# Two tiles for a blocked inverse, and a merge step put in another order, in a two-layer AdaLN kernel

## What is computed

```python
h = layernorm(x) * (1 + ca) + sa
qkvz = h @ W_qkvz                       # per key head: q, k, 2 v, 2 z of 128 columns
q, k, v = silu(causal_conv4(q, k, v))   # four taps along the sequence
beta = sigmoid(b); alpha = exp(-exp(A_log) * softplus(a + dt_bias))
q, k = l2norm(q) / sqrt(128), l2norm(k)
def step(S, q_t, k_t, v_t, a_t, b_t):   # scan over 256 positions
    S = S * a_t
    v_new = (v_t - S^T k_t) * b_t
    S = S + outer(k_t, v_new)
    return S, S^T q_t
og = o * silu(z)
og = og * rsqrt(mean(og * og) + 1e-6) * norm_weight
x = x + ga * (og @ W_out)
```

## Time and profile before

| | us |
|---|---|
| median of 3 runs | 1217.29 (1217.04 to 1225.51) |
| profiled execution | 1213.53 |
| its span in the trace | 1211.8 |
| PE busy | 1089.0 (90%) |
| DVE busy | 957.2 (79%) |
| ACT busy | 808.4 (67%) |
| POOL busy | 733.3 (61%) |

### The profile page before, as it was taken

The page is one execution under the profiler, slowest core; times in us unless marked ns, Lnnn a source line. Parts: engine busy times, 40 slices in busy tenths (PEclk is TensorE's granted clock), DMA queues, the critical chain, the costliest instruction groups (busy, mean ns, idle before and its releaser), DMA issues. The chain is left out here.

```text
span 1211.8 us, 29974 instructions
## 1 busy us (share of the span) xinstructions
PE 1089.0 (90%) x10488; PEld 948.9 (78%) x10488; DVE 957.2 (79%) x2560; ACT 808.4 (67%) x2225; POOL 733.3 (61%) x1186
## 2 busy tenths in 40 slices
PE   6684799999999999999999999999998888999985
PEld 6583688988888888889898888888887776776754
DVE  6888689898989899999989898989982435328754
ACT  6342576777777777877777777777775764219873
POOL 3274677777777776787778777777777512014111
PEclk9886999999999999999999999999998999999988
DMA  5221226323131313132222313131314130011000
GB/s 186 65 60 36 86 48 73 58 67 80 45 90 41 82 43 106 35 90 56 68 57 68 90 41 83 41 82 33 72 39 126 34 105 1 1 37 39 2 19 18
DMA packets 140869, 72.79 MB, mean 60 GB/s; under 512 B 114184, under 2 KB 130064, under 8 KB 138800
## 3 DMA queue, kind: packets, MB, share of 16 engines
q1 hardware_dynamic: 140720, 70.88, 23.0%
HBM read 57.06 MB, written 13.78 MB: 58 GB/s over the span
## 5 line engine op out<-in xcount | busy, mean ns | idle before, releaser
L1076 POOL TENSOR_TENSOR Tn<-Tn,tmp 64x31 f32<-64x31 f32 (+15 forms) x496 | 280.3, 565 | 38.9
L1073 POOL TENSOR_TENSOR tmp<-DT,Tn 64x31 f32<-64x31 f32 (+15 forms) x496 | 251.6, 507 | 49.4 <-DMA DT<-blk_in_scratch 15.3
L866 DVE SCALAR_TENSOR_TENSOR cv<-bank,cw,cv 128x255 f32<-128x255 f32 (+2 forms) x384 | 155.1, 472 | 52.4 <-ACT cv L665 52.3
L866 DVE SCALAR_TENSOR_TENSOR cqk<-bank,cw,cqk 128x255 f32<-128x255 f32 (+2 forms) x384 | 154.9, 471 | 26.7 <-ACT cqk L665 26.7
L1049 POOL TENSOR_TENSOR ro<-ss,mhalf 128x4 f32<-128x4 f32 x64 | 68.6, 1072 | 130.9 <-issue 76.4
L935 DVE SCALAR_TENSOR_TENSOR BP<-bank,cj,E 128x512 f32<-128x512 f32 (+1 forms) x256 | 144.6, 611 | 2.5 <-DVE cj L916 0.3
L476 PE MATMUL bank<-wo,OTs 128*128 128x256 f32 x512 | 136.2, 394 | 1.5 <-ACT OTs L758 1.5
L727 ACT ACTIVATE junk<-og 128x129 f32<-128x129 f32 x256 | 79.4, 310 | 53.2 <-issue 41.7
L476 PEld LDWEIGHTS bank<-wo,OTs 128*128 128x128 f32 x512 | 89.9, 193 | 13.0 <-ACT OTs L758 2.0
L735 ACT ACTIVATE ogn<-og,ro 128x128 f32<-128x128 f32 x256 | 81.9, 396 | 21.3 <-POOL ro L1049 20.4
L315 PE MATMUL bank<-hh,wqk_hi 128*128 128x256 f32 x256 | 79.0, 309 | 14.8 <-DVE wqk_lo L885 11.2
(11 more groups left out here) (211 smaller groups left out, 3249.2 us busy)
## 6 DMA issues: line engine op xcount, KB each, us to landing
rvz<-in_L_attn_W_qkvz SPq DMA_DIRECT2D x16, 512.0 KB, 3.6
x<-alpha_scratch SPq DMA_DIRECT2D x8, 1024.0 KB, 5.6
alb<-alpha_scratch SPq DMA_DIRECT2D x7, 1024.0 KB, 4.7
rqk<-in_L_attn_W_qkvz SPq DMA_DIRECT2D x16, 256.0 KB, 2.6
wo<-in_L_attn_W_out SPq DMA_DIRECT2D x16, 256.0 KB, 3.6
blk_in_scratch<-BP SPq DMA_DIRECT2D x256, 16.0 KB, 1.5
DT<-blk_in_scratch SPq DMA_DIRECT2D x16, 256.0 KB, 3.5
tinv_scratch<-Tn SPq DMA_DIRECT2D x32, 128.0 KB, 2.2
```

The source lines that it names most:

```text
L866: nc.vector.scalar_tensor_tensor(d, bk[:, t * T:(t + 1) * T - s], cw[p][:, first + t, TAPS - 1 - s:TAPS - s], d, ALU.mult, ALU.add).then_i ...
L1073: pool_step_done(nc.gpsimd.tensor_tensor(t, Dm[:, j, j + 1:BLK].unsqueeze(2).broadcast_to([SLOTS, r, c]), Tn[:, j, 0:c].unsqueeze(1).broad ...
L1076: pool_step_done(nc.gpsimd.tensor_tensor(Tn[:, j + 1:BLK, 0:c], Tn[:, j + 1:BLK, 0:c], t, ALU.subtract), kh * NTS + 2 * j + 4)
```

## The change

- Tn and tmp take 128 partitions in place of 64. Key heads take turns: an even one has partitions 0 to 63 of DT, Tn and tmp, an odd one 64 to 127 (`own`). The turned inverse is written over the blocks in DT of the same key head. The tiles are cleared and given their diagonal once, ahead of the loop; from the third key head on, one affine_select clears what lies above the diagonal. The counts of the semaphore t_step follow (`t_base`, `t_rows`).
- GpSimd's waits for the store and the turn before a new inverse are for the inverse two key heads back.
- Rows by step: 0 to 13, 14 to 16, 17 to 23, 24 to 30.
- wqk's split: ScalarE's half stays at the end of the merge step; the low half goes from VectorE to GpSimd, behind ro and the power of vsc. wvz's split, now for two key heads ahead: ScalarE's half in step 1 behind SiLU of v and in front of the squares; VectorE's half at the end of step 3.
- The squares of the merge step's og stand behind Y in step 1 in place of in front of it.
- VectorE's scans in the merge step: two long ones in front of `dve_acc`, then R, two short ones, two long ones, og. In step 1 two short ones in front of R and a long one behind it, in step 2 the last three.
- `bet`, a copy of beta's two columns for a key head, is gone; cj reads beta.
- GpSimd waits for ro, vsc's power and its split before it goes on.

```diff
+            Tn = sb("Tn", [2 * SLOTS, BLK, BLK], ctx=s1)
+            tmp = sb("tmp", [2 * SLOTS, 256], ctx=s1)
+            def own(tile, kh):
+                return tile[kh % 2 * SLOTS:(kh % 2 + 1) * SLOTS]
+            def t_base(kh):
+                return kh * 2 * (BLK - 1) + max(kh - 2, 0)
+            def t_rows(kh, rows):
+                return t_base(kh) + (1 if kh >= 2 else 0) + 2 * rows
...
             def act_step(kh, p, b):
-                if last and merges(last[2]):
-                    act_ss(*last)
                 if merges(b):
...
-                    splits(kh, p, b, act_split_qk, act_split_vz)
+                    if kh + 3 < NKH:
+                        act_split_qk(kh + 3, 1 - p)
                 else:
                     act_y(kh, p, b, 0)
+                    if merges(last[2]):
+                        act_ss(*last)
...
                     if vz:
                         act_silu_v(*vz)
+                    if b == 1 and kh + 2 < NKH:
+                        act_split_vz(kh + 2, p)
                     act_ss(kh, p, b)
...
             def dve_step(kh, p, b):
-                if gram and gram[2] == 0:
-                    dve_bet(gram[0], gram[1])
...
                 if not merges(b):
                     if b == 1:
-                        scans_ahead(2, 0, R)
+                        scans_ahead(1, R)
                     dve_r2(kh, p, b)
-                    if b == 2:
-                        scans_ahead(1, R, 2 * R)
+                    if b == 1:
+                        scans_ahead(2, 0, 1)
+                    elif b == 2:
+                        scans_ahead(1, 1)
...
+                if merges(b):
+                    scans_ahead(1, 0, R)
                 if last:
                     dve_acc(*last)
                 if merges(b):
-                    scans_ahead(1)
                     dve_r2(kh, p, b)
-                    scans_ahead(2)
-                    splits(kh, p, b, dve_split_qk, dve_split_vz)
+                    scans_ahead(1, R)
+                    scans_ahead(2, 0, R)
                     dve_og(kh, p, b)
+                if b == B - 1 and kh + 2 < NKH:
+                    dve_split_vz(kh + 2, p)
...
-            SPLIT = ((0, 14), (14, 18), (18, 25), (25, BLK - 1))
+            SPLIT = ((0, 14), (14, 17), (17, 24), (24, BLK - 1))
+            def pool_split_qk(kh, p):
+                wait(nc.gpsimd, "wqk_high", kh + 1)
+                nc.gpsimd.tensor_tensor(wqk[p][1][:], rqk[:], wqk[p][0][:].bitcast(F32), ALU.subtract).then_inc(sem("wqk_split"), 1)
...
             def pool_inverse_start(kh):
-                wait(nc.gpsimd, "t_out0", kh * 32)
-                wait(nc.gpsimd, "t_turned", 2 * kh)
-                pool_step_done(nc.gpsimd.memset(Tn[:], 0.0), kh * NTS + 1)
-                pool_step_done(nc.gpsimd.affine_select(out=Tn[:], in_=Tn[:], compare_op=ALU.not_equal, fill=1.0, base=0,
-                                                       pattern=[[1, BLK], [-1, BLK]], channel_multiplier=0), kh * NTS + 2)
+                T = own(Tn, kh)
+                wait(nc.gpsimd, "t_out0", (kh - 1) * 32)
+                wait(nc.gpsimd, "t_turned", 2 * (kh - 1))
+                pool_step_done(nc.gpsimd.affine_select(out=T, in_=T, compare_op=ALU.is_ge, fill=0.0, base=0,
+                                                       pattern=[[-1, BLK], [1, BLK]], channel_multiplier=0), t_rows(kh, 0))
...
             def pool_step(kh, p, b):
...
                 pool_ro(kh, p, b)
+                wait(nc.gpsimd, "ro", at(kh, b, 1, 1))
                 if b == 0 and kh + 1 < NKH:
                     pool_vpow(kh + 1, 1 - p)
+                    wait(nc.gpsimd, "vpow", kh + 2)
+                if b == 0 and kh + 3 < NKH:
+                    pool_split_qk(kh + 3, 1 - p)
+                    wait(nc.gpsimd, "wqk_split", kh + 4)
...
             def sp_blocks_turn(kh):
...
-                wait(nc.sync, "t_step", kh * NTS)
-                nc.sync.dma_start(Dm.rearrange("s j i -> s (j i)"), ...)
+                wait(nc.sync, "t_step", t_base(kh - 1))
+                wait(nc.sync, "t_out1", (kh - 1) * 32)
+                nc.sync.dma_start(own(DT, kh).rearrange("s j i -> s (j i)"), ...)
```

More of the change, by code:

```diff
@@ L219, in build @@
             cw = [sb(f"cw{p}", [P, 4, TAPS], ctx=s1) for p in range(2)]
-            bet = [sb(f"bet{p}", [P, NT, R], ctx=s1) for p in range(2)]
             nw = sb("nw", [P, 1], ctx=s1)
@@ L747, in act_turn @@
             def act_turn(kh, half):
-                wait(nc.scalar, "t_step", kh * NTS + (2 + BLK - 2 if half == 0 else NTS))
-                wait(nc.scalar, "t_out1", kh * 32)
+                wait(nc.scalar, "t_step", t_rows(kh, BLK // 2 - 1 if half == 0 else BLK - 1))
+                wait(nc.scalar, "t_out1", (kh - 1) * 32)
                 rows = slice(half * BLK // 2, (half + 1) * BLK // 2)
-                nc.scalar.activation(Tt[:, :, rows], Tn[:, rows, :].rearrange("s j i -> s i j"), ACT.Copy).then_inc(sem("t_turned"), 1)
+                nc.scalar.activation(own(DT, kh)[:, :, rows], own(Tn, kh)[:, rows, :].rearrange("s j i -> s i j"), ACT.Copy).then_inc(sem("t_turned"), 1)
             def act_ots(kh, p, b):
@@ L889, in dve_split_vz @@
                 nc.vector.tensor_tensor(wvz[p][1][:], rvz[:], wvz[p][0][:].bitcast(F32), ALU.subtract).then_inc(sem("wvz_split"), 1)
[L891 to L900, removed]
             def dve_scales(kh, p, b):
@@ L914, in dve_scales @@
                 wait(nc.vector, "rcn", at(kh, b, 1, 1))
-                wait(nc.vector, "bet", kh + 1)
-                nc.vector.tensor_tensor(cj[i][:], bet[p][:, NC * b:NC * (b + 1), :], rcn[i][:].unsqueeze(2).broadcast_to([P, NC, R]),
+                nc.vector.tensor_tensor(cj[i][:], beta[:, NC * b:NC * (b + 1), kh * R:(kh + 1) * R], rcn[i][:].unsqueeze(2).broadcast_to([P, NC, R]),
                                         ALU.mult).then_inc(sem("cj"), 1)
@@ L1059, in pool_inverse_start @@
             def pool_inverse_start(kh):
[L1060 to L1064 removed]
+                T = own(Tn, kh)
[3 more added lines that the diff above has]
+                                                       pattern=[[-1, BLK], [1, BLK]], channel_multiplier=0), t_rows(kh, 0))
             def pool_inverse(kh, lo, hi):
[L1068 removed]
+                D, T, tk = own(DT, kh), own(Tn, kh), own(tmp, kh)
+                if lo == 0:
                     wait(nc.gpsimd, "blk_in", (kh + 1) * 16)
@@ L1130, in sp_blocks_turn @@
                     wait(nc.sync, f"blk_dr{b}", (kh + 1) * 16 * NBLK)
-                wait(nc.sync, "t_step", kh * NTS)
-                nc.sync.dma_start(Dm.rearrange("s j i -> s (j i)"), blkin_dr.rearrange("n b c h j i -> (n b c h) (j i)")).then_inc(sem("blk_in"), 16)
+                wait(nc.sync, "t_step", t_base(kh - 1))
+                wait(nc.sync, "t_out1", (kh - 1) * 32)
+                nc.sync.dma_start(own(DT, kh).rearrange("s j i -> s (j i)"), blkin_dr.rearrange("n b c h j i -> (n b c h) (j i)")).then_inc(sem("blk_in"), 16)
             def sp_blocks_out(kh, i):
-                dr, src = ((tinv_dr, Tn[:]), (ttin_dr, Tt))[i]
+                dr, src = ((tinv_dr, own(Tn, kh)), (ttin_dr, own(DT, kh)))[i]
                 if i == 0:
-                    wait(nc.sync, "t_step", (kh + 1) * NTS)
+                    wait(nc.sync, "t_step", t_base(kh + 1))
                 else:
@@ L1555, in _ @@
                     b = g - B
-                    if b == 0:
-                        dve_bet(1, 1)
                     if g == 2 * B:
@@ L1619, in _ @@
                 n = 0
-                for t, v in ((ones[:], 1.0), (npow[:, 0:2], -0.5), (npow[:, 2:4], 0.5),
+                for t, v in ((Tn[:], 0.0), (ones[:], 1.0), (npow[:, 0:2], -0.5), (npow[:, 2:4], 0.5),
                              (og[:, :, :, DK:DK + 1], (DK * DK * 1e-6) ** 0.5)):
```

22 lines of the change are left out of this document (9 added, 13 removed).

## The result

The changed kernel took 1222.28 us (median of 20 runs) against 1216.54 for the kernel before: ratio 1.0047, 95% interval 1.0033 to 1.0061. I had forecast 1216 with the sign the other way (-1.3 us). The profiled execution has a span of 1218.9 us against 1211.8.

The account below looks back on a forecast made before the run. Bound: the loop's period, TensorE nearly always busy and the inverse's line with 0.47 us to spare. Forecast: -0.1 us in each of twelve periods, -1.3 us, edges 0, so 1212.2 profiled, median 1216; range 1196 to 1228.

Parts of the forecast that it names:

- The edges: First key head and last three, outside the twelve steady periods: put at 0, bounds 2 us either way.
- The gain of 1.3 us: Sum over the loop: period 55.96 against a mean of 56.07, -0.1 us in each of twelve periods.
- Off the line: Preparation ahead of the loop: beta's copies and the tile's clearing at the start were claimed to cost no time.
- Y first: Step 1: Y copied before the squares; squares 1.4 us earlier, the 1.26 us wait gone, TensorE waiting 0.7 for ogn.
- Seven rows behind it: Inverse rows behind step 2's ro: row 24 adds 1.16 us, inverse ends at 54.1 against 53.68, next Gram at 55.96.
- TensorE sets the period: Rival, chance 0.22: inverse ends by 52.4, so TensorE's own work makes the period 54.3; 21 us less, 1196.
- Two inverse tiles: GpSimd no longer waits 2.67 us for the old inverse's store or clears for 0.94; worth nothing by itself, up to 0.5.
- DMA order: SyncE's queue: the next wvz load issues earlier but nobody waited for it, block loads come no earlier; no gain.
- Split on GpSimd: wqk's low half on GpSimd behind vpow: taken as 1.57 us, bounds 1.05 to 3.1, done at 34.3 in the period.
- vpow holds the port: Rival, chance 0.05: step 1's scans wait for vpow on the shared port, 2.4 us a period, 29 us more, 1245.
- The wait for Y stays: Rival, chance 0.06: first solve's product, not order, held Y; only R's 0.68 gained, 7 us more, 1224.

Follow-up runs that it names:

- one row there: Changed kernel with one inverse row moved up into the merge step (rows 0-15, 15-19, 19-26, 26-31): 1194.58 us, ratio 0.9785 to the kernel before.
- Y first alone: Kernel before with one move, the copy of Y in front of the squares of the merge step's gated outputs: 1231.6 us, ratio 1.0107.
- two tiles alone: Kernel before with only the two inverse tiles, beta read in place and GpSimd's new waits for ro and vsc's power: 1216.07 us, ratio 0.998.
- two rows put back: Changed kernel with inverse rows 17 and 24 back where they were (14-18, 18-25, 25-31): 1201.66 us, ratio 0.9857 to the kernel before.

## Why the prediction was wrong

**The edges: the step that failed.** "The first key head (it starts late) and the last three (fewer products) I put at 0, bounds 2 us either way." Key heads 0, 13 and 14 cost 6.6 us together (mean of two traces, 175.7, against mean of three, 169.1): 1.5, 2.2 and 2.9. The steady periods gave 2.3 (12 x 0.19). The rest is +4.3 us, and the two comparisons measured 5.7 and 4.3.

The reason is one that my sum held already. It had the inverse's end 0.4 us later (row 24 in its last stretch, for an earlier ro), and in the loop this fitted into the 0.47 us that the inverse had to spare in front of the turn. At the edges that slack was 0.14 us (key head 0) and none (key head 13, where the turn already waited). In key head 0 (first trace of each kernel) ro of step 1 and 2 come 0.3 and 0.8 later than before, row 24 adds its 1.2, and the inverse ends at 54.92 us behind the merge copy instead of 52.81; the turn, which waited for nothing there, now waits 1.8. In key head 13 no Gram opens the next merge step, and what ends it is the merge itself, which needs the inverted blocks. Now ScalarE waits for the inverse, where its turn waited 0.55 before:

```profile
908.69 1.16 ACT L761 ACTIVATE DT<-Tn 64x512 f32<-64x512 f32 x1 [2.52 <-POOL Tn L1084]
```

Behind that turn stand the store and load of the blocks (SyncE's queue, the kernel before, then the changed one), and behind them the merge. TensorE stands in front of it, and its clock is low when it runs (timeline, then windows of TensorE, changed kernel):

```profile
906.18 1.54 SPq L1151 DMA_DIRECT2D U<-tinv_scratch  x3
...
911.65 1.51 SPq L1165 DMA_DIRECT2D U<-tinv_scratch  x3
```

```profile
912.65 0.35 PE L353 MATMUL bank<-hh,wvz_hi 128*128 128x256 f32 x1 [2.28 <-ACT hT L689]
...
915.20 0.23 PE L399 MATMUL bank<-U,BP 32*32 32x32 f32 x1 [1.60 <-issue]
```

```profile
905.00:912.00 7.00, 4.79 (x32) 1.00 0.32 63
912.00:917.00 5.00, 2.74 (x70) 0.73 0.78 167
917.00:922.00 5.00, 5.00 (x113) 0.50 0.06 8
```

Counted from the merge copy that opens key head 13, the inverse ends 1.0 us later, the blocks are asked for at 50.2 instead of 48.8, and the merge starts at 53.7 instead of 52.2. Then the diagonal merge takes 1.95 us from its first matmul to the copy of A, against 1.30 before (909.59 to 910.89). These 1.5 and 0.65 are the 2.2 us. The stand of 2.28 in front of the projection costs nothing by itself: TensorE comes there 1.0 us earlier than before, and the copy it waits for stands where it stood (50.5 and 50.3). I had named the slack of a steady period as the number to decide on, and never read it for the first and the last ones, where TensorE has less to do and that slack is smaller.

Key head 14 is the largest part and the one least explained. Its length goes with the clock in it: 54.96, 53.11 and 53.59 us at mean granted clocks of 0.90, 0.94 and 0.94 in the kernel before, 55.69 and 57.87 at 0.90 and 0.85 in the changed one. But one row there has 0.87 and 54.70 although its key head 13 is short, and in the first trace of the kernel before the clock falls there too (0.50 over the window 912 to 917). So how much of these 2.9 us the two rows cost, and how much the clock would have taken anyway, stays open.

**The gain of 1.3 us: right in size, for another reason.** It came from setting a period built up from one that I had read (55.96) against the mean of twelve (56.07); the period that I had read took 55.96 as well. The mean is higher because of one period of 57.28 (744.09 to 801.37), where TensorE stood 2.12 us for Y and then ran at the lower clock (timeline, then window of TensorE, kernel before):

```profile
763.79 1.20 PE L442 MATMUL bank<-Y,BP 128*128 128x128 f32 x4 [2.12 <-ACT Y L699]
```

```profile
764.00:767.00 3.00, 3.00 (x15) 0.50 0.09 17
```

The three traces of the kernel before have such a fall in 6 of their 36 periods, the two of the changed kernel in none of 24. Without these six the mean period is 56.03 in both kernels. So the new order by itself gained nothing in a period, as my line by line account had it, and the 0.19 is what the falls had cost, a term that the sum did not have. That it met the forecast is luck.

**The preparation.** "Off the line" was neither shown nor refuted. 3.5 of the 7.1 us between the two profiled spans stand there, but the same preparation takes 122.8, 123.0 or 127.0 in the kernel before and 127.4 in Y first alone, and two tiles alone, which has the changed preparation and a first copy at 127.3, is not slower than the kernel before. All ten traces with the changed preparation lie at 126.5 or above, though; whether it takes the longer course more often, and so holds a part of the 5.7 us, stays open.

**Y first.** The period that I had read was not the usual one: in eight of twelve TensorE stands 1.7 us for Y, in three 2.1, there 1.26. And the 1.94 us of ScalarE end at t = 23.96, they do not begin there; the sum used them rightly. The station was right (squares at t = 22.8, forecast 22.6; ogn's wait 0.85, forecast 0.7), the credit was not. I wrote that og comes earlier than Y is copied, and did not ask what follows: the squares, the start of the inverse's line, then wait for a solve that they do not need. The gain of 1.4 us that I gave to this part belongs to the splits and R moved off VectorE's tail; Y first itself costs 1.0 us a period, 12 of the 16 us by which the ratios of the two kernels differ (1.0047 and 0.9915).

**Seven rows behind it.** Right: "what the earlier ro gave is spent on the row". The line stations came out at 35.9, 47.0 and 54.5 or 54.0, the period at 55.95 (55.96), the Gram's wait at 1.6 (1.6).

**TensorE sets the period.** 54.3 was a fair figure for its own work with the wait for ogn (54.07 once the inverse is out of the way), and this rival's condition, an inverse that ends earlier, was near: two rows put back left 0.4 us a period of the Gram's wait, and a third row moved took that away. The 1194.58 of one row there is close to the rival's 1196.

**Two inverse tiles, DMA order.** Put at nothing; worth 0.2 us a period in the loop beside the periods without a fall of the clock (55.85 against 56.03), and 2.4 us over all, with an interval that reaches no change. **Split on GpSimd.** 1.27 us, not 1.57, and hidden: GpSimd stands 1.4 us idle behind it. **vpow holds the port.** No: see the last section. **The wait for Y stays.** No, it is gone from TensorE's waits.

## What to carry to other kernels

When a change makes a second line the longest one by tenths, look for the stretches where the first line is shorter (first and last rounds): the second line is paid for there in full. Before an operation is moved in front of another on an engine, compare when the inputs of the two are ready after the whole change, not before it. And an idle piece in front of a station is worth something only if the work that goes into it makes room for work from behind the last station; move rows along the line together. Last, set a period that was worked out from one period against that same period, and look at what pulls the mean away from it.

## What the runs showed of the hardware

With Y first alone, stands of 1.6 to 2.4 us in one piece in front of ogn's transposes brought TensorE from 2.4 to 1.2 GHz for about 3 us in nine of twelve periods; three stands of 2.0 us did not. In the three traces of the kernel before, six of the ten stands of 2.1 us in front of the second solve did so, and none of the 26 of 1.2 to 1.7 us. 1.5 to 1.8 us in front of the Gram did not in the changed kernel, whose granted clock is 1.00 over all twelve periods. A stand of the same length can have two prices, and what decides between them these runs do not show.

VectorE's scans depend on what GpSimd does beside them (timeline of VectorE, changed kernel; GpSimd runs rows of the inverse until 371.8, vpow from 376.7 to 379.7, and stands idle from 406.8 to 410.0):

```profile
370.25 2.07 DVE L889 TENSOR_TENSOR_SCAN E<-alb,eye 128x256 f32<-128x256 f32 x2
...
377.19 0.69 DVE L889 TENSOR_TENSOR_SCAN E<-alb,eye 128x256 f32<-128x256 f32 x1
...
408.47 1.27 DVE L889 TENSOR_TENSOR_SCAN E<-x,eye 128x256 f32<-128x256 f32 x2
```

A pair of long scans takes 1.27 us with GpSimd idle, just as it took inside vpow before the change, and 2.07 mostly beside the rows. Over the twelve periods of the changed kernel the median record of one long scan is 0.68 us with GpSimd idle (23 scans), 0.68 inside vpow (12) and 1.02 where rows fill over nine tenths of it (49). So vpow does not hinder a scan at all, while the rows, each instruction a fraction of a us long, do. The Trainium skill, "SBUF — State Buffer", section "SBUF: two separate sides", has the two engines' shared ports locked for a whole instruction of either; the scan inside vpow disagrees here as it did before the change. Beside the rows a wait for part of a row would lengthen the record as well as a slower scan would, and the traces do not tell the two apart.
